# Cross attention and a top-4 expert layer on one core: the expert loop unrolled to 16 blocks a turn, with its stages two steps apart

## The chip, the cores and the metric

The kernel runs on one core of one Trainium2 chip (trn2). The metric is the device time of one execution in microseconds (us); lower is better. A change is told as a ratio of two such times.

## The reference, cut to what matters

The input is `x` of 4 x 1024 tokens with 256 features in float32, and a context of 4 x 77 tokens. One layer of cross attention (16 heads) is added to `x`; then comes the part that matters here, a feed-forward layer with 32 experts, of which each token picks 4, and one expert shared by all:

```python
T = B * S                                   # 4096 tokens
scores = softmax(xf @ Wg)                   # over E = 32 experts
weights, indices = top_k(scores, 4)
for e in range(E):
    tok, w = the tokens that chose e, and their weights      # at most 2048
    xg = xf[tok]
    out = silu(xg @ W1[e]) * (xg @ W3[e]) @ W2[e] * w[:, None]
    y = y.at[tok].add(out)
z = silu(xf @ Ws1) * (xf @ Ws3) @ Ws2
return x + y + z
```

Here D = 256, the inner width H = 128, and `W1`, `W3` are 256 x 128, `W2` is 128 x 256 for each expert. All matmuls are in float32, which the compiler splits, so that one product of 128 x 128 by 256 columns is two instructions on TensorE.

## The kernel before, in words

The kernel is written engine by engine: each engine has its own program, and they meet through counting semaphores alone. It has four parts in time: weights of the attention are folded together (up to about 165 us); attention, the second normalization, the router and the sending of each token's row into lists in HBM, one list per expert (to about 550 us); the shared expert, partly in between (to 584 us); and then two parts that matter here, the expert loop (586.6 to 888 us) and the sum of the four expert rows of each token (891 to 954 us).

**The expert loop** works on blocks of 128 rows of the lists, `BLOCKS` = 160 of them; which rows and which expert a block has stands in a table `tab` of three rows in SBUF (first row of the list, expert, column with the row numbers). One block passes these stages:

- SyncE loads the block's 128 rows from the list (`load_turn`, L525) into `xblk[:, q]`, one of `NX` = 8 buffers, 144 KB.
- TensorE transposes it (`block_T`, two transposes, L1235), and VectorE copies the result to `xbT` (`move_xbT`, L1186) and the 128 target row numbers to `yrow[:, q]` (L1188), which also has 8 columns.
- TensorE multiplies with `W1` and `W3` of the expert (`block_up`, four matmul instructions, L1467). ScalarE takes the silu of one half (`silu`, L831, into `eg`), VectorE multiplies with the other (`gate`, L1195, into `eh`).
- TensorE transposes `eh` (`block_hT`, L1235), VectorE copies it to `ehT` (`move_ehT`, L1202).
- TensorE multiplies with `W2` (`block_down`, two matmul instructions, L1481), ScalarE copies the result to `eo` (`move_eo`, L836), 8 buffers, and GpSimd sends its 128 rows of 1 KB by an indirect DMA to the rows `yrow` of `y_d` in HBM (`scatter_block`, L659).

So a block takes 9 matmul instructions on TensorE, each with a load of its weights.

**The order of the work** is written out by hand, by the helper `turns` (L319 to L332). Every engine runs through steps; in step q TensorE does `block_T` of block q, `block_up` of block q-1, `block_hT` of block q-2 and `block_down` of block q-3 (`LAG` = 3). VectorE does, in a step, `move_xbT` of q, `move_ehT` of q-2, `gate` of q-1; ScalarE does `silu` of q-1 and `move_eo` of q-3. A turn has `NX` = 8 steps. Turn 0 is written out, the turns 1 to 19 are a hardware loop (`Fori`), and the rest of the last blocks is written out behind it, so TensorE passes the end of a turn 20 times.

The transposed and intermediate buffers `xbT`, `eg`, `eh`, `ehT` have two copies each, and each stage has two of the eight PSUM banks. `move_xbT` of block b waits, through the semaphore `scattered[q]`, until the indirect DMA of block b-8 has landed, since `yrow` and `xblk` have eight places; `move_eo` waits for the same DMA, since `eo` has eight places. SyncE loads block b into `xblk` once block b-8 has been transposed and its row numbers copied.

In its turns 1 to 8, after the eight loads of the turn, SyncE also loads 512 KB of the shared expert's output from HBM (`base`, L536), which the final sum needs. Turn 9 is a loop of its own and so are the turns after it.

Of the kernel before, what the change touches and what calls it, by code (L numbers as in the profile page):

```python
# [17 lines left out]
I32 = mybir.dt.int32  # L18
U32 = mybir.dt.uint32
# [4 lines left out]
P = 128  # L24
# [6 lines left out]
def attention_moe_kernel(nc, x, ctx, Wq, bq, Wk, bk, Wv, bv, Wo, bo, gamma, beta,  # L31
# [46 lines left out]
    with ExitStack() as stack:  # L78
# [85 lines left out]
        tabf = sb("tabf", [P, 2, 3])  # L164
        tab = sb("tab", [3, LAG + BLOCKS + NX], I32)
        p1 = ExitStack()
# [151 lines left out]

        def turns(eng, stages, order, load_turn=None):  # L319

            def turn(i, qs, skip):
                of_turn = load_turn(i) if load_turn else None
                for q in qs:
                    for lag in order:
                        if not skip(q, lag):
                            stages[lag](i + (q - lag) // NX, (q - lag) % NX, of_turn and of_turn(q, lag))
# [64 lines left out]
        def _(sp):  # L392
# [125 lines left out]
            sp.wait_ge(s["tab_ready"], 1)  # L518
            rows_of = table(sp, "first_row", 0, LAG + NX, DUMMY)
# [23 lines left out]
            for q in range(NX):  # L543
                sp.wait_ge(scattered[q], 16 * TURNS)

# [23 lines left out]
        def _(pool):  # L569
# [93 lines left out]
            for q in range(NX):  # L663
                scatter_block(0, q)
            with pool.Fori(1, TURNS) as i:
                for q in range(NX):
                    scatter_block(i, q)
# [40 lines left out]
        def _(act):  # L708
# [117 lines left out]

            def silu(i, q, _):
# [5 lines left out]
            def move_eo(i, q, _):  # L833
                wait(act, scattered[q], i * 16)
                wait(act, "eo_psum", i * NX + (q + 1))
# [29 lines left out]
        def _(dve):  # L865
# [314 lines left out]

            def move_xbT(i, q, col):
                b = i * NX + q
# [3 lines left out]
                nc.vector.tensor_copy(xbT[:, q % 2, :, :].rearrange("p k n -> p (k n)"), bank(q % 2)[:, 0:D]  # L1186
                                      ).then_inc(s["xbT_sbuf"], 1)
                nc.vector.tensor_copy(yrow[:, q:q + 1], xblk[:, q, bass.ds(col, 1)].bitcast(U32)  # L1188
                                      ).then_inc(s["yrow_ready"], 1)

            def gate(i, q, _):
                b = i * NX + q
                wait(dve, "ehT_psum", b - 1)
                wait(dve, "eg_ready", b + 1)
                nc.vector.tensor_tensor(eh[:, q % 2, :], eg[:, q % 2, :], bank(2 + q % 2)[:, H:2 * H], ALU.mult  # L1195
                                        ).then_inc(s["eh_ready"], 1)

            def move_ehT(i, q, _):
                b = i * NX + q
                wait(dve, "eo_psum", b - 1)  # L1200
                wait(dve, "ehT_psum", b + 1)
                nc.vector.tensor_copy(ehT[:, q % 2, :], bank(4 + q % 2)[:, 0:P]).then_inc(s["ehT_sbuf"], 1)  # L1202

            turns(dve, {0: move_xbT, 1: gate, 2: move_ehT}, (0, 2, 1), table(dve, "y_col", 2, LAG + NX, ROW - 1))

# [24 lines left out]
        def _(pe):  # L1230
# [222 lines left out]

            def block_T(i, q, _):
                b = i * NX + q
                wait(pe, "xbT_sbuf", b - 1)
                wait(pe, ld_x[q], (i + 1) * 16)
                for k in range(KC):
                    last = transpose(bank(q % 2)[:, k * P:(k + 1) * P], xblk[:, q, k * P:(k + 1) * P])
                last.then_inc(s["xbT_psum"], 1)  # L1460

            def block_up(i, q, e):
                b = i * NX + q
                wait(pe, "eh_ready", b - 1)
                wait(pe, "xbT_sbuf", b + 1)
                for k in range(KC):
                    last = mm(bank(2 + q % 2)[:, 0:2 * H], xbT[:, q % 2, k, :],  # L1467
                              ew[:, bass.ds(e, 1), k * 2 * H:(k + 1) * 2 * H], start=k == 0, stop=k == KC - 1)
                last.then_inc(s["eh_psum"], 1)

            def block_hT(i, q, _):
                b = i * NX + q
                wait(pe, "ehT_sbuf", b - 1)
                wait(pe, "eh_ready", b + 1)
                transpose(bank(4 + q % 2)[:, 0:P], eh[:, q % 2, :]).then_inc(s["ehT_psum"], 1)

            def block_down(i, q, e):
                b = i * NX + q
                wait(pe, "eo_ready", b - 1)
                wait(pe, "ehT_sbuf", b + 1)  # L1480
                mm(bank(6 + q % 2)[:, 0:D], ehT[:, q % 2, :], ew[:, bass.ds(e, 1), 2 * D:3 * D], start=True, stop=True  # L1481
                   ).then_inc(s["eo_psum"], 1)
# [30 lines left out]
```

## Time and profile before

| what | value |
|---|---|
| time, median of 3 runs | 955.42 us |
| the 3 runs | 952.56, 4682.61, 955.42 us |
| the profiled execution: its span, first to last instruction of the program | 954.6 us |
| expert loop, from TensorE's first transpose to the end of the last indirect DMA's issue | 586.6 to 889.3 us |
| final sum | 891 to 954 us |

The table's first two lines are times without the profiler; for the profiled execution the page gives its span and no other time, and the span is 0.8 us below the median of the runs. PE is TensorE's matmul side, PEld its weight loads; a q behind an engine's name marks its sequencer (PEldq is TensorE's). A row of the timeline gives start, duration, engine, line, operation, names, count and, in brackets, the idle time before and what ended it; several like instructions can be merged into one row.

### The profile page before, as it was taken

To read this page: it belongs to the slowest core of one execution; us is meant where nothing else is said; L and a number is where in the kernel's file an instruction comes from. 1 tells how busy PE (TensorE), PEld (TensorE's weight loads), DVE (VectorE), ACT (ScalarE), POOL (GpSimd) and SP (SyncE) were. 2 spreads that over 40 slices of the span, in tenths; PEclk is the share of its full clock that TensorE was granted. 3 is DMA by queue.
4 is the path that set the end of the run, shared out by engine and by line. 5 is a ranking of instruction groups with operands and counts; after the bars stand their busy time and mean duration, and the time that the engine had idled before them with its cause. 6 is when DMAs were issued, how large, how long until landed. Compare 5 with 4: busy or idle time off the path is not lost.

```text
span 954.6 us, 17750 instructions
## 1 busy us (share of the span) xinstructions
PE 811.0 (85%) x3822; PEld 579.6 (61%) x3823; DVE 537.7 (56%) x1753; ACT 406.1 (43%) x1661; POOL 400.4 (42%) x397
## 2 busy tenths in 40 slices
PE   7877999999999999999689997898898898988100
PEld 4654666666666666666545655777777777777000
DVE  1763226667666767676847223555555555555588
ACT  1444767575757575757231111333333333333000
POOL 1201122247473737373852810455555545555100
PEclk9989999999999999999969999999999999999655
DMA  6245222234342425694393963656554444443799
GB/s 223 90 123 172 78 78 78 101 109 168 106 172 102 174 102 175 203 309 146 118 368 127 317 236 123 192 179 190 185 185 146 157 146 141 162 142 112 233 366 303
DMA packets 134396, 163.17 MB, mean 171 GB/s; under 512 B 11765, under 2 KB 121283, under 8 KB 134339
## 3 DMA queue, kind: packets, MB, share of 16 engines
q1 hardware_dynamic: 118595, 117.97, 39.7%
q0 software_dynamic: 15744, 44.62, 12.2%
q14 instruction: 43, 0.35, 0.1%
q8 instruction: 14, 0.23, 0.1%
HBM read 84.25 MB, written 78.27 MB: 170 GB/s over the span
## 4 chain that ended last, share of the span: by engine, by line
PE 73%; DMA 7%; DVE 7%; issue 5%; ACT 5%; SPq 0%; DVEq 0%; POOL 0%; POOLq 0%; ACTq 0%
PE psum L1321 15%; PE psum L1467 15%; PE psum L1235 11%; PE psum L1364 11%; PE psum L1481 7%; PE psum L1402 5%; ACT sm L768 4%; PE psum L1323 3%; DMA big<-y_d 3%; PE psum L1413 2%; DMA big<-in_x 2%; PE psum L1385 2%; DVE big L1217 2%; DMA pT<-xn2T_d 1%; DVE st L869 1%
## 5 line engine op out<-in xcount | busy, mean ns | idle before, releaser
L659 POOL DMA_INDIRECT y_d<-sm,yrow x160 | 155.1, 970 | 180.7 <-DVE yrow L1188 158.1
L1467 PE MATMUL psum<-big,xbT 128*128 x640 | 167.8, 385 | 1.3 <-DVE eh L1195 1.1
L1321 PE MATMUL psum<-big,xnT 128*128 (+2 forms) x384 | 157.2, 533 | 3.6 <-ACT sm L768 3.0
L768 ACT ACTIVATE sm<-psum,nmax 128x77 f32<-128x77 f32 x512 | 157.4, 371 | 0.0
L636 POOL DMA_INDIRECT expert_lists<-rows,slot x128 | 126.2, 986 | 59.4 <-issue 38.6
L618 POOL TENSOR_TENSOR sm<-sm,sinv 128x1232 f32<-128x1232 f32 x32 | 72.0, 2248 | 179.6 <-DVE sinv L1100 179.4
L1364 PE MATMUL psum<-big,pT 128*128 (+1 forms) x640 | 145.1, 383 | 2.0 <-DVE res L1091 2.0
L1364 PEld LDWEIGHTS psum<-big,pT 128*128 128x128 f32 x640 | 120.5, 192 | 17.0 <-DVE res L1091 2.1
L768 ACT ACTIVATION_READ_ACCUMULATOR sm<-psum,nmax 128x1 f32 x512 | 130.1, 254 | 0.1
L1467 PEld LDWEIGHTS psum<-big,xbT 128*128 128x128 f32 x640 | 109.7, 192 | 12.8 <-issue 2.3
L831 ACT ACTIVATE eg<-psum 128x128 f32<-128x128 f32 x160 | 44.4, 278 | 151.3 <-PE psum L1467 151.3
L1186 DVE COPY xbT<-psum 128x256 f32<-128x256 f32 x160 | 68.0, 425 | 57.7 <-PE psum L1235 46.5
L1481 PE MATMUL psum<-big,ehT 128*128 x320 | 95.7, 381 | 0.1
L1202 DVE COPY ehT<-psum 128x128 f32<-128x128 f32 x160 | 46.7, 292 | 85.5 <-PE psum L1235 83.9
L1321 PEld LDWEIGHTS psum<-big,xnT 128*128 128x128 f32 x384 | 65.9, 191 | 47.4 <-issue 42.3
L1235 PE MATMUL psum<-ident,xblk 128*128 128x128 f32 x320 | 62.5, 278 | 30.9 <-issue 30.9
L836 ACT ACTIVATE sm<-psum 128x256 f32<-128x256 f32 x160 | 61.3, 383 | 50.8 <-PE psum L1481 50.8
L1076 DVE TENSOR_REDUCE nmax<-psum 128x12 f32<-128x924 f32 x64 | 50.5, 794 | 53.1 <-PE psum L1323 53.0
L1235 PEld LDWEIGHTS psum<-ident,xblk 128*128 128x128 f32 x320 | 43.9, 142 | 52.9 <-issue 39.1
L1402 PE MATMUL psum<-pT,ws 128*128 128x512 f32 x128 | 64.0, 653 | 7.8 <-DMA pT<-xn2T_d 6.9
L1481 PEld LDWEIGHTS psum<-big,ehT 128*128 128x128 f32 x320 | 48.4, 191 | 12.4 <-issue 0.5
L1402 PEld LDWEIGHTS psum<-pT,ws 128*128 128x128 f32 x128 | 26.4, 210 | 38.5 <-issue 35.3
(181 smaller groups left out, 1061.5 us busy)
## 6 DMA issues: line engine op xcount, KB each, us to landing
xblk<-expert_lists SPq DMA_DIRECT2D x160, 144.0 KB, 2.2
y_d<-zero SPq DMA_DIRECT2D x32, 512.0 KB, 3.5
big<-y_d SPq DMA_DIRECT2D x32, 512.0 KB, 8.0
big<-in_L_ffn_W SPq DMA_DIRECT2D x16, 320.0 KB, 5.9
xin<-in_x SPq DMA_DIRECT2D x36, 128.0 KB, 2.1
expert_lists<-filler POOLq DMA_DIRECT2D x32, 144.0 KB, 3.9
big<-in_x SPq DMA_DIRECT2D x8, 512.0 KB, 3.5
xres<-in_x SPq DMA_DIRECT2D x8, 512.0 KB, 4.8
```

The source lines that it names most:

```text
L618: pool.tensor_tensor(e3, e3, sinv[:, t % 2, :].unsqueeze(2).to_broadcast([P, NH, SK]), ALU.mult).then_inc(s["probs_ready"], 1)
L636: pool.indirect_dma_start(out=lists, out_offset=bass.IndirectOffsetOnAxis(ap=slot[:, ph, tt, k:k + 1], axis=0), in_=rows[:, ph, tt, :], in ...
L659: pool.indirect_dma_start(out=y_d, out_offset=bass.IndirectOffsetOnAxis(ap=yrow[:, q:q + 1], axis=0), in_=eo[:, q, :], in_offset=None).the ...
L768: last = nc.scalar.activation(sm[:, t % 2, h * SK:(h + 1) * SK], head_scores(h, h + 1), ACT.Exp, bias=nmax[:, t % 2, h:h + 1], accum_out=s ...
L836: nc.scalar.activation(eo[:, q, :], bank(6 + q % 2)[:, 0:D], ACT.Copy).then_inc(s["eo_ready"], 1)
L1186: nc.vector.tensor_copy(xbT[:, q % 2, :, :].rearrange("p k n -> p (k n)"), bank(q % 2)[:, 0:D]).then_inc(s["xbT_sbuf"], 1)
L1235: return nc.tensor.transpose(out, in_, ident[0:n, 0:n])
L1321: mm(head_scores(h0, h1), xnT[:, t % 2, k, :], A[:, k, bass.ds(b, 1), cols], start=k == 0, stop=False)
L1364: last = mm(o_ps[:, 0:D], pT[:, to % 2, c, :], VO[:, bass.ds(batch(jo, po), 1), c, :], start=c == 0, stop=c == CK - 1)
L1402: last = mm(bank(2 * n + c), ws13[:, k, n * HS + c * P:n * HS + (c + 1) * P], xg[:, p, k, :], start=k == 0, stop=k == KC - 1)
L1467: last = mm(bank(2 + q % 2)[:, 0:2 * H], xbT[:, q % 2, k, :], ew[:, bass.ds(e, 1), k * 2 * H:(k + 1) * 2 * H], start=k == 0, stop=k == KC - 1)
L1481: mm(bank(6 + q % 2)[:, 0:D], ehT[:, q % 2, :], ew[:, bass.ds(e, 1), 2 * D:3 * D], start=True, stop=True).then_inc(s["eo_psum"], 1)
```

## The change

The steps of a turn become 16 and the stages are put two steps apart: `block_up` is done of block q-2, `block_hT` of block q-4 and `block_down` of block q-6 (`LAG` = 6). `xbT`, `eh` and `ehT` get four copies (`NB4`); `xblk`, `yrow`, `eo` keep eight, `eg` and the PSUM banks two. The waits for the reuse of `xbT`, `eh` and `ehT` are loosened accordingly. The table load takes `LAG + NTURN` = 22 registers. ScalarE and GpSimd keep turns of 8. TensorE, VectorE and SyncE now have 10 turns: turn 0 written out, 1 to 9 in loops. SyncE's `base` loads stay one per turn, in turns 1 to 8. The diff, cut to its core:

```diff
-    LAG = 3
-    TURNS = BLOCKS // NX
+    AT_UP, AT_HT, LAG = 2, 4, 6
+    NB4 = 4
+    NTURN = 16
+    TURNS = BLOCKS // NTURN
...
-        xbT = sb("xbT", [P, 2, KC, P])
+        xbT = sb("xbT", [P, NB4, KC, P])
         eg = sb("eg", [P, 2, H])
-        eh = sb("eh", [P, 2, H])
-        ehT = sb("ehT", [P, 2, P])
+        eh = sb("eh", [P, NB4, H])
+        ehT = sb("ehT", [P, NB4, P])
...
-            turn(0, range(NX), lambda q, lag: q < lag)
-            with eng.Fori(1, TURNS) as i:
-                turn(i, range(NX), lambda q, lag: False)
-            turn(TURNS, range(LAG), lambda q, lag: q >= lag)
+            turn(0, range(n), lambda q, lag: q < lag)
+            with eng.Fori(1, BLOCKS // n) as i:
+                turn(i, range(n), lambda q, lag: False)
+            turn(BLOCKS // n, range(LAG), lambda q, lag: q >= lag)
...
-                eng.reg_load(regs, tab[row:row + 1, bass.ds(i * NX, n)])
+                eng.reg_load(regs, tab[row:row + 1, bass.ds(i * NTURN, n)])
...
-                for q in range(NX):
-                    wait(sp, "xbT_psum", (i - 1) * NX + (q + 1))
-                    wait(sp, "yrow_ready", (i - 1) * NX + (q + 1))
-                    sp.dma_start(xblk[:, q, :], lists[bass.ds(of_turn(q, 0), P), :]).then_inc(ld_x[q], 16)
+                for q in range(NTURN):
+                    wait(sp, "xbT_psum", i * NTURN + (q + 1 - NX))
+                    wait(sp, "yrow_ready", i * NTURN + (q + 1 - NX))
+                    sp.dma_start(xblk[:, q % NX, :], lists[bass.ds(of_turn(q, 0), P), :]).then_inc(ld_x[q % NX], 16)
...
-            turns(act, {1: silu, LAG: move_eo}, (1, LAG))
+            turns(act, {AT_UP: silu, LAG: move_eo}, (AT_UP, LAG), NX)
...
-            def move_xbT(i, q, col):
-                b = i * NX + q
-                wait(dve, "eh_psum", b - 1)
-                wait(dve, scattered[q], i * 16)
+            def move_xbT(b, q, col):
+                x = q % NX
+                wait(dve, "eh_psum", b + (1 - NB4))
+                wait(dve, scattered[x], (b - x) * (16 // NX))
                 wait(dve, "xbT_psum", b + 1)
...
-                wait(dve, "ehT_psum", b - 1)
+                wait(dve, "ehT_psum", b + (1 - NB4))
...
-                wait(dve, "eo_psum", b - 1)
+                wait(dve, "eo_psum", b + (1 - NB4))
...
-            turns(dve, {0: move_xbT, 1: gate, 2: move_ehT}, (0, 2, 1), table(dve, "y_col", 2, LAG + NX, ROW - 1))
+            turns(dve, {0: move_xbT, AT_UP: gate, AT_HT: move_ehT}, (0, AT_HT, AT_UP), NTURN, table(dve, "y_col", 2, LAG + NTURN, ROW - 1))
...
-            turns(pe, {0: block_T, 1: block_up, 2: block_hT, LAG: block_down}, (0, 1, 2, LAG),
-                  table(pe, "expert", 1, LAG + NX, E - 1))
+            turns(pe, {0: block_T, AT_UP: block_up, AT_HT: block_hT, LAG: block_down}, (0, AT_UP, AT_HT, LAG), NTURN,
+                  table(pe, "expert", 1, LAG + NTURN, E - 1))
```

The waits that are not shown (`scattered` at the end of SyncE's part, the counts in `silu` and `move_eo`) name the same events in the new count of blocks.

## Rows read from the trace of the kernel before

**Rows 1.** Stretch view, one turn: span, PE, PEld, DVE, ACT, POOL (count), clock, DMA.
```profile
688.50:703.35 14.85, 13.38 (x73) 10.96 (x72) 7.79 (x33) 5.29 (x16) 7.75 (x9) 1.00 0.59 185
```

**Rows 2.** Chain that ended last, around two turn ends: start, us, what.
```profile
703.37 1.46 issue
704.83 0.43 PE psum L1235 x2
...
718.21 1.41 issue
```

**Rows 3.** Sequencers, by line: ns min/median/max, first and last start.
```profile
L330 PEldq ALU_OP  x1: 32/32/32, 702.3 to 702.3; - x1
...
L339 PEldq TENSOR_LOAD <-tab x21: 1376/1526/2186, 584.2 to 880.6; - x21
L339 SPq TENSOR_LOAD <-tab x20: 1147/1204/1582, 569.2 to 851.9; - x20
...
L647 POOLq TENSOR_LOAD <-fill_at x4: 1038/1084/1327, 523.9 to 544.9; - x4
...
L340 PEldq FUSED_REGOPS  x21: 85/180/180, 586.4 to 882.2; - x21
```

**Rows 4.** Timeline of one step on PE, DVE and ACT, and the next step's start.
```profile
699.95 0.38 PE L1235 MATMUL psum<-ident,xblk 128*128 128x128 f32 x2
...
700.37 0.43 DVE L1186 COPY xbT<-psum 128x256 f32<-128x256 f32 x1
...
701.62 0.28 DVE L1195 TENSOR_TENSOR eh<-eg,psum 128x128 f32<-128x128 f32 x1
...
701.58 0.38 PE L1235 MATMUL psum<-ident,xblk 128*128 128x128 f32 x2
...
701.84 0.38 ACT L836 ACTIVATE sm<-psum 128x256 f32<-128x256 f32 x1 [0.33 <-PE psum L1481]
```

**Rows 5.** Timeline of POOL, and the landing of the DMA issued at 694.88.
```profile
694.88 0.97 POOL L659 DMA_INDIRECT y_d<-sm,yrow  x1 [0.60 <-DVE yrow L1188]
...
703.07 0.97 POOL L659 DMA_INDIRECT y_d<-sm,yrow  x1 [0.66 <-DVE yrow L1188]
...
DMA to landing us min/median/max: 2.4/2.4/2.4
```

**Rows 6.** Timeline of SP and POOL at a `base` load; landings of L536 and of 688.22.
```profile
688.49 0.40 SPq L536 DMA_DIRECT2D base<-base_d  x1
...
688.22 0.97 POOL L659 DMA_INDIRECT y_d<-sm,yrow  x1 [0.66 <-DVE yrow L1188]
...
DMA to landing us min/median/max: 4.6/4.6/4.7
...
DMA to landing us min/median/max: 4.7/4.7/4.7
```

**Rows 7.** TensorE's clock: an idle stretch on PE and the stretch after it.
```profile
555.58 0.99 PE L1402 MATMUL psum<-pT,ws 128*128 128x512 f32 x1 [2.02 <-DMA pT<-xn2T_d]
...
555.80:559.20 3.40, 3.40 (x5) 1.34 (x5) 0.00 (x0) 0.00 (x0) 0.00 (x0) 0.51 0.86 322
```

**Rows 8.** Ends of a turn in two other loops: DVE's branches, next instructions, instructions a turn.
```profile
262.50:358.70 96.20, 95.63 (x453) 64.77 (x452) 65.77 (x197) 63.95 (x315) 54.20 (x43) 1.00 0.40 137
...
L303 DVEq COMPARE_BRANCH  x1: 63/63/63, 358.7 to 358.7; - x1
...
361.60 0.29 DVE L986 TENSOR_REDUCE lmax<-logits 128x4 f32<-128x128 f32 x1 [2.75 <-ACT logits L790]
...
921.60:935.90 14.30, 0.00 (x0) 0.00 (x0) 12.85 (x33) 0.00 (x0) 0.00 (x0) 0.50 1.10 366
...
L1224 DVEq FUSED_REGOPS  x1: 70/70/70, 921.8 to 921.8; - x1
```

**Rows 9.** Timeline of POOL, the last two indirect DMAs.
```profile
887.01 0.97 POOL L659 DMA_INDIRECT y_d<-sm,yrow  x1 [0.49 <-ACT sm L836]
888.29 0.97 POOL L659 DMA_INDIRECT y_d<-sm,yrow  x1 [0.30 <-issue]
```

More of the change, by code:

```diff
@@ L164, in attention_moe_kernel @@
         tabf = sb("tabf", [P, 2, 3])
-        tab = sb("tab", [3, LAG + BLOCKS + NX], I32)
+        tab = sb("tab", [3, LAG + BLOCKS + NTURN], I32)
         p1 = ExitStack()
@@ L317, in shared_rest, with turns @@
                     step(i, p)
-        def turns(eng, stages, order, load_turn=None):
+        def turns(eng, stages, order, n, load_turn=None):
             def turn(i, qs, skip):
@@ L326, in turn @@
                         if not skip(q, lag):
[L327 to L332 removed]
+                            stages[lag]((i + (q - lag) // n) * n + (q - lag) % n, (q - lag) % n,
+                                        of_turn and of_turn(q, lag))
+            turn(0, range(n), lambda q, lag: q < lag)
+            with eng.Fori(1, BLOCKS // n) as i:
+                turn(i, range(n), lambda q, lag: False)
+            turn(BLOCKS // n, range(LAG), lambda q, lag: q >= lag)
         def table(eng, name, row, n, max_val):
@@ L664, in _ @@
                 scatter_block(0, q)
-            with pool.Fori(1, TURNS) as i:
+            with pool.Fori(1, BLOCKS // NX) as i:
                 for q in range(NX):
@@ L831, in silu, with move_eo @@
                 nc.scalar.activation(eg[:, q % 2, :], bank(2 + q % 2)[:, 0:H], ACT.Silu).then_inc(s["eg_ready"], 1)
-            def move_eo(i, q, _):
-                wait(act, scattered[q], i * 16)
-                wait(act, "eo_psum", i * NX + (q + 1))
+            def move_eo(b, q, _):
+                wait(act, scattered[q], (b - q) * (16 // NX))
+                wait(act, "eo_psum", b + 1)
                 nc.scalar.activation(eo[:, q, :], bank(6 + q % 2)[:, 0:D], ACT.Copy).then_inc(s["eo_ready"], 1)
-            turns(act, {1: silu, LAG: move_eo}, (1, LAG))
+            turns(act, {AT_UP: silu, LAG: move_eo}, (AT_UP, LAG), NX)
         def rsqrt(dve, name, base, var, eps, w):
@@ L1452, in _, with block_T, block_up @@
             pe.wait_ge(s["z_added"], 2 * NG)
-            def block_T(i, q, _):
-                b = i * NX + q
+            def block_T(b, q, _):
+                x = q % NX
                 wait(pe, "xbT_sbuf", b - 1)
-                wait(pe, ld_x[q], (i + 1) * 16)
+                wait(pe, ld_x[x], (b - x) * (16 // NX) + 16)
                 for k in range(KC):
-                    last = transpose(bank(q % 2)[:, k * P:(k + 1) * P], xblk[:, q, k * P:(k + 1) * P])
+                    last = transpose(bank(q % 2)[:, k * P:(k + 1) * P], xblk[:, x, k * P:(k + 1) * P])
                 last.then_inc(s["xbT_psum"], 1)
-            def block_up(i, q, e):
-                b = i * NX + q
+            def block_up(b, q, e):
                 wait(pe, "eh_ready", b - 1)
@@ L1466, in block_up, with block_hT, block_down @@
                 for k in range(KC):
-                    last = mm(bank(2 + q % 2)[:, 0:2 * H], xbT[:, q % 2, k, :],
+                    last = mm(bank(2 + q % 2)[:, 0:2 * H], xbT[:, q % NB4, k, :],
                               ew[:, bass.ds(e, 1), k * 2 * H:(k + 1) * 2 * H], start=k == 0, stop=k == KC - 1)
                 last.then_inc(s["eh_psum"], 1)
-            def block_hT(i, q, _):
-                b = i * NX + q
+            def block_hT(b, q, _):
                 wait(pe, "ehT_sbuf", b - 1)
                 wait(pe, "eh_ready", b + 1)
-                transpose(bank(4 + q % 2)[:, 0:P], eh[:, q % 2, :]).then_inc(s["ehT_psum"], 1)
-            def block_down(i, q, e):
-                b = i * NX + q
+                transpose(bank(4 + q % 2)[:, 0:P], eh[:, q % NB4, :]).then_inc(s["ehT_psum"], 1)
+            def block_down(b, q, e):
                 wait(pe, "eo_ready", b - 1)
                 wait(pe, "ehT_sbuf", b + 1)
-                mm(bank(6 + q % 2)[:, 0:D], ehT[:, q % 2, :], ew[:, bass.ds(e, 1), 2 * D:3 * D], start=True, stop=True
+                mm(bank(6 + q % 2)[:, 0:D], ehT[:, q % NB4, :], ew[:, bass.ds(e, 1), 2 * D:3 * D], start=True, stop=True
                    ).then_inc(s["eo_psum"], 1)
-            turns(pe, {0: block_T, 1: block_up, 2: block_hT, LAG: block_down}, (0, 1, 2, LAG),
-                  table(pe, "expert", 1, LAG + NX, E - 1))
+            turns(pe, {0: block_T, AT_UP: block_up, AT_HT: block_hT, LAG: block_down}, (0, AT_UP, AT_HT, LAG), NTURN,
+                  table(pe, "expert", 1, LAG + NTURN, E - 1))
 TAB_OPS = 21
```

21 lines of the change are left out of this document (9 added, 12 removed).

## Prediction

> **What bounds the kernel now.** I read the page first: TensorE is the busiest engine, and the chain that ended last runs through it for most of the span, in the expert loop for all of it. So the loop's turns come next. A turn of 8 blocks [rows 1] has TensorE's matmuls busy for 13.38 of 14.85 us at clock 1.00; VectorE has 7.79, so no other engine is near a bound. The chain [rows 2] shows one hole a turn: 1.46 us of "issue", where TensorE waits for no other engine; from one hole's start to the next it is 718.21 - 703.37 = 14.84 us. Inside a turn TensorE has no hole: the transposes of two neighbouring blocks start at 699.95 and 701.58 [rows 4], 1.627 us apart (steps of 1.62 and 1.63 alternate), and PE isn't idle between them. So a step is TensorE's own work, and a turn's end costs 14.84 - 8 x 1.627 = 1.82 us, a little more than the hole, and 20 ends cost 36.4 us. What fills the hole is on TensorE's sequencer [rows 3]: it counts the loop at 702.3, branches, loads 11 registers (1.526 us, median) and computes with them (0.180 us); the first weight load comes about 2.5 us behind 702.3. About 0.7 us of this is hidden by what was handed over before.
>
> **Turn ends, part by part.** The change has 10 ends instead of 20. Each load now takes 22 registers. The trace has no such load, so I bound it: GpSimd loads 8 in 1.084 us and SyncE 11 in 1.204 [rows 3], 0.04 us for each further register, which gives +0.44 for 11 more; in proportion to the count it would be +1.53. I take 0.06 a register, nearer to the row with the slope, so +0.66, and for L340 +0.13 (0.180 for 11, 0.085 in the last turn, where three are used, so 0.012 a register): +0.79 in all, bounds +0.57 and +1.7. The hand-over gains 0.2 us, as worked out below. An end then costs 1.82 + 0.79 - 0.2 = 2.4, ten cost 24: **-12.4 us** (bounds -14 to -3).
>
> The Trainium skill has a dearer rule (Runtime: NRT & Kernel Launch, Instruction fetch mechanics): about 200 ns for each register loaded, even in bulk. The trace disagrees at 11 registers, 1.526 us where the rule gives 2.2. By the rule's slope 11 more would be +2.2 us and ten ends some 15 us more than in my sum.
>
> **The stages two steps apart.** Inside a turn TensorE is already full, so spacing can't speed up a step. It could bring something at a turn's end alone: the sequencer could run further ahead. What it does to the ring of 8 buffers, which stays, is worse. In a step whose transposes start at 0 (699.95), VectorE copies `xbT` at 0.42, `gate` ends at 1.95, `move_eo` ends at 2.27 [rows 4], and the indirect DMA starts at 3.12 (703.07) and lands 2.4 later, at 5.5 [rows 5]. The copy of block b waits for the landing of block b-8. Before, block b-8 has its step of `block_down` at b-5, so the landing is at 5.5 and the copy at 5 x 1.627 + 0.42 = 8.55: 3.05 us to spare (rows 5 and 4: issued at 694.88, landed 697.3, copy of the eighth block after it at 700.37). With `LAG` = 6 that step is at b-2: the copy could be at 2 x 1.627 + 0.42 = 3.67, but the landing is at 5.5. Every copy is 1.83 us late. Two steps of spacing nearly absorb this. Step b+2 needs, before its `block_up`, `gate` of b-2, which VectorE does behind the late copy: 5.5 + 0.1 to start, 1.0 for copy, row numbers, `ehT` and `gate` (700.37 to 701.9 without its waits), 0.1 and 0.25 for the sequencer is 6.95 from the start of step b-2. That must fit in 4 steps and 0.2: 4P = 6.75, P = 1.69 instead of 1.627. Where the turn's end lies within the four steps it gives the time back, so I count 12 of 16 steps in 9 turns: 108 x 0.06 = **+6.5 us** (bounds 0 and +14). As `gate` comes that late, the sequencer is held as before and gains only 0.2 us at the end of a turn; without the ring it would gain 1.3 (its last wait would be for `move_eo` of two steps ago, 2 x 1.627 - 2.27 = 0.98 us ahead of the step's start, instead of for the last `gate`, 1.95 - 1.627 = 0.32 us behind it).
>
> **What was hidden by the 3.05 us.** In eight turns a 512 KB `base` load lies in the queues for 4.6 us, and the indirect DMA beside it lands after 4.7 instead of 2.4 [rows 6]. Before, 3.05 + the turn's end covered that. Now there is no spare, and the base load is issued in the middle of a turn (right behind the load that waits for the row numbers of the turn's block 7), while two indirect DMAs are under way or start; the later landing, +1.0 to +2.3 us, goes straight into TensorE. 8 x 1.5 = **+12 us** (bounds 0 and +18).
>
> **Start, end, clock.** The first table load lies open (TensorE starts with it): +0.8. At the end, the last blocks' `block_down` come 0.54 us apart, but GpSimd needs 887.01 to 888.29 = 1.28 for each indirect DMA [rows 9]; with six blocks instead of three to drain, the last is issued some 1.2 us later: together **+2 us**. The granted clock is 1.00 with holes of 1.46 us [rows 1, 2]. After a hole of 2.02 us it was 0.5 (1.2 of 2.4 GHz) for 3.4 us [rows 7], which costs 1.7. The new hole is 1.46 + 0.79 - 0.2 = 2.05. I take that it falls at two or three of ten ends: **+4 us** (bounds 0 and +17). SyncE's own end of turn and its later stores of `base` run 8 blocks (13 us) ahead and cost nothing; VectorE's own load starts about a step behind TensorE's, and two steps of cover absorb that. Eight and four buffers in SBUF cost no time.
>
> **Sum.** -12.4 + 6.5 + 12 + 2 + 4 = +12.1 us on a span of 954.6: 966.7, or on the median, 0.8 higher, **967.5 us**.
>
> **Rivals.**
> - B, the ring doesn't bind: the landing comes earlier than the trace says, or the copy isn't held. Then the sequencer's lead of 1.3 counts: ten ends of 1.82 + 0.79 - 1.3 = 1.31, saving 36.4 - 13.1 = 23.3, less 2 for start and end: 955.4 - 21.3 = 934.1. For it: the purpose of two steps of cover. Against: rows 4 and 5 leave no room for 6 steps and a landing in 8.
> - C, the ring binds but `base` loads don't hit (the delayed landing falls on a block with cover from the turn's end): 967.5 - 12 = 955.5. For it: the hit depends on tenths of a us; against: two indirect DMAs start in any 3.3 us.
> - D, slower by over 2%: the turn's end decides. Above a hole of about 2 us the clock falls at every end, 10 x 1.7 = 17 instead of 4, and with the hits at 2 us (+16 instead of 12) it is 984.5. It begins to win where the load of 22 registers takes over about 2.3 us.
> - E, the longer body doesn't stay in the instruction store: at the end of a turn of the attention loop (197 VectorE instructions a turn) VectorE branches at 358.7 and starts its next instruction at 361.60, 2.75 us idle; in the final sum (33 a turn) the next sequencer instruction starts 0.2 us behind the branch [rows 8]. The new body has 64, nearer to 33. If it missed, 9 x 2.75 = 25 more: 992. TensorE's body of 144 matmuls is below the 453 of the attention turn, which shows no hole.
>
> The Trainium skill's rule here (same page and section) is that a branch to a page that is no longer in the engine's small window waits for a fetch; the VectorE rows agree that there is such a wait of some 2.7 us, and leave open from which size.
>
> **Chances.** A (forecast) 0.43, of which 0.05 above 974.5; B 0.07; C 0.22; D 0.23; E 0.05. The kernel's measurement can tell about 2% (19 us) from no change: faster 0.07 (B), same 0.38 + 0.22 = 0.60, slower 0.05 + 0.23 + 0.05 = 0.33. The range, 947 to 987, leaves out B and most of E.
>
> **What would show it.** 10 holes of about 2 us on TensorE instead of 20 of 1.46; TENSOR_LOAD of 2.2 us; steps of `block_T` at 1.627 with some longer ones, mean near 1.69; VectorE's `xbT` copy starting 2.2 us, not 0.42, after the transposes, released by the indirect DMA; a step of over 3 us in the middle of turns 1 to 8 and none in turn 9; 0.5 in the clock behind some ends. Steps of 1.627 throughout and a copy at 0.42 would refute the ring; mid-turn holes missing, the hits.

## The result, and the profile after

The changed kernel takes 978.94 us (median of four runs, 976.60 to 980.12), the kernel before 955.66 us on the same chip (median of four, one of which, 4682.61 us, is far from the rest). The ratio is 1.025, with a 95% interval of 1.0228 to 1.0271: slower by 23.3 us, about twice the 12 us forecast, and above the 2% that the prediction took as what can be told from no change.

The profiled execution has a span of 978.1 us against 954.6. First its page: busy time by engine, the chain that ended last, and the costliest group on VectorE.

```profile
PE 829.8 (85%) x3822; PEld 586.9 (60%) x3823; DVE 523.6 (54%) x1753; ACT 406.5 (42%) x1661; POOL 401.2 (41%) x397
...
PE 56%; DMA 17%; issue 9%; DVE 8%; ACT 6%; POOL 3%; DVEq 1%; POOLq 1%; SPq 1%; ACTq 0%
PE psum L1321 15%; PE psum L1364 11%; DMA y_d<-sm,yrow 9%; PE psum L1235 8%; PE psum L1466 7%; PE psum L1402 4%; ACT sm L771 4%; POOL y_d L662 3%; DMA big<-y_d 3%; PE psum L1323 3%; PE psum L1478 3%; DMA big<-in_x 2%; PE psum L1413 2%; PE psum L1385 2%; DVE big L1217 1%
...
L1188 DVE COPY xbT<-psum 128x256 f32<-128x256 f32 x160 | 67.7, 423 | 166.8 <-DMA y_d<-sm,yrow 121.2
```

The reader is to see `DMA y_d<-sm,yrow` in the chain with 9% of the span. VectorE was idle for 166.8 us ahead of the 160 copies of `xbT`, and 121.2 of them ended with the landing of an indirect DMA. In the kernel before the same group (there L1186) reads:

```profile
L1186 DVE COPY xbT<-psum 128x256 f32<-128x256 f32 x160 | 68.0, 425 | 57.7 <-PE psum L1235 46.5
```

The stretch view answers to [rows 1]; its columns are the same. These are two neighbouring turns of 16 blocks, 31.70 and 30.62 us, where two turns of 8 took 29.7.

```profile
644.87:676.57 31.70, 28.46 (x145) 21.76 (x145) 13.86 (x64) 10.60 (x32) 15.99 (x17) 1.00 0.51 162
676.57:707.19 30.62, 27.85 (x144) 21.97 (x145) 14.11 (x64) 10.59 (x32) 15.56 (x17) 1.00 0.49 158
```

The sequencers' table loads, now of 22 registers, answer to [rows 3]:

```profile
L342 PEldq TENSOR_LOAD <-tab x11: 1934/2040/2210, 581.7 to 899.8; - x11
L342 SPq TENSOR_LOAD <-tab x10: 1620/1880/2131, 567.5 to 856.7; - x10
```

The timeline around a `base` load answers to [rows 4 to 6]. To be seen: each copy of `xbT` is ended by the DMA, and starts 0.76 to 0.92 us behind the transposes of the next block, where it used to start 0.42 behind its own. At 692.20 the `base` load goes out, VectorE then stands idle for 1.74 us, the copy at 695.29 starts 3.4 us behind its transposes, and TensorE's next transposes wait for it.

```profile
689.37 0.42 DVE L1188 COPY xbT<-psum 128x256 f32<-128x256 f32 x1 [1.01 <-DMA y_d<-sm,yrow]
...
690.08 0.38 PE L1235 MATMUL psum<-ident,xblk 128*128 128x128 f32 x2
690.84 0.42 DVE L1188 COPY xbT<-psum 128x256 f32<-128x256 f32 x1 [0.60 <-DMA y_d<-sm,yrow]
...
692.20 0.40 SPq L539 DMA_DIRECT2D base<-base_d  x1
692.67 0.42 DVE L1188 COPY xbT<-psum 128x256 f32<-128x256 f32 x1 [0.95 <-DMA y_d<-sm,yrow]
...
695.29 0.42 DVE L1188 COPY xbT<-psum 128x256 f32<-128x256 f32 x1 [1.74 <-DMA y_d<-sm,yrow]
695.77 0.44 PE L1235 MATMUL psum<-ident,xblk 128*128 128x128 f32 x2 [0.41 <-DVE xbT L1188]
```

In the next turn the same hit is larger, and the granted clock falls behind it (timeline, then the stretch at 0.50):

```profile
723.45 0.40 SPq L539 DMA_DIRECT2D base<-base_d  x1
...
728.05 0.42 DVE L1188 COPY xbT<-psum 128x256 f32<-128x256 f32 x1 [3.43 <-DMA y_d<-sm,yrow]
728.54 0.44 PE L1235 MATMUL psum<-ident,xblk 128*128 128x128 f32 x2 [2.10 <-DVE xbT L1188]
```

```profile
729.51:732.92 3.41, 3.41 (x12) 2.59 (x11) 1.57 (x8) 0.66 (x2) 0.00 (x0) 0.50 0.51 142
```

A turn's end, on TensorE's timeline, with its hole of 2.15 us, answers to [rows 2]. The bracket names a copy of VectorE, but TensorE's sequencer is in its table load until 706.4 and computes with the registers until 706.9:

```profile
704.44 0.60 PE L1478 MATMUL psum<-big,ehT 128*128 x2
707.19 0.43 PE L1235 MATMUL psum<-ident,xblk 128*128 128x128 f32 x2 [2.15 <-DVE xbT L1188]
```

**Where the 23 us are.** A step is the time from a block's transposes to the next block's; a full one is 1.63 us. From the first block's transposes to the last block's the kernel before takes 293.0 us and the changed one 314.65. Summing what each step has above 1.63 us by its place in the turn gives, in us (step 0 goes from the transposes of a turn's first block to those of its second; an end is step 15 with steps 0 and 1 behind it, in turns of 8 step 7 with those two):

| | before | after | difference |
|---|---|---|---|
| turns' ends (19; 9), without falls of the clock | 34.5 | 21.6 | -12.9 |
| steps 2 to 9, 13 and 14 of a turn | 0 | 7.9 | +7.9 |
| steps 10 to 12 (place of the `base` load), without falls | 0 | 15.7 | +15.7 |
| six falls of the clock, three at ends, three in steps 10 to 12, 1.75 each | 0 | 10.5 | +10.5 |
| first turn, rounding | -0.7 | -0.3 | +0.4 |
| last transposes to last indirect DMA | 8.6 | 12.9 | +4.3 |
| start of the loop's first block | 586.6 | 584.2 | -2.4 |

The sum is +23.5 us. The final sum behind the last indirect DMA is the same in both, 66.3 us. The 1.75 us for a fall is an estimate from turns' ends with and without one, below. The parts repeat, the falls do not: a second trace of the changed kernel (`after_again`, below) has by the same sums 21.6 us at ends, 9.8 in steps 2 to 9, 13 and 14, 15.6 in steps 10 to 12, and four falls instead of six, 7.0 us.

Of the 15.7 us, 3.4 stand in turn 7, at block 122, together with one of the falls. An experiment below shows that these stay when the `base` load of that turn is moved away. The `base` loads of the other turns thus go with 12.1 us and two falls (turn 9, which has no such load, has the other 0.2).

### The profile page after: what moved, and what is told of

Its sections match the earlier page's. It is cut to its first block, busy times and chain, and to the rows that moved or that the text cites. A ratio compares the mean times of both kernels' runs of the same rounds, so it can differ in the third digit from the quotient of the medians.

```text
span 978.1 us, 17716 instructions
## 1 busy us (share of the span) xinstructions
PE 829.8 (85%) x3822; PEld 586.9 (60%) x3823; DVE 523.6 (54%) x1753; ACT 406.5 (42%) x1661; POOL 401.2 (41%) x397
## 4 chain that ended last, share of the span: by engine, by line
PE 56%; DMA 17%; issue 9%; DVE 8%; ACT 6%; POOL 3%; DVEq 1%; POOLq 1%; SPq 1%; ACTq 0%
PE psum L1321 15%; PE psum L1364 11%; DMA y_d<-sm,yrow 9%; PE psum L1235 8%; PE psum L1466 7%; PE psum L1402 4%; ACT sm L771 4%; POOL y_d L662 3%; DMA big<-y_d 3%; PE psum L1323 3%; PE psum L1478 3%; DMA big<-in_x 2%; PE psum L1413 2%; PE psum L1385 2%; DVE big L1217 1%
## 5 line engine op out<-in xcount | busy, mean ns | idle before, releaser
L1466 PE MATMUL psum<-big,xbT 128*128 x640 | 177.1, 401 | 3.7 <-DVE eh L1196 1.5
L1188 DVE COPY xbT<-psum 128x256 f32<-128x256 f32 x160 | 67.7, 423 | 166.8 <-DMA y_d<-sm,yrow 121.2
L1364 PEld LDWEIGHTS psum<-big,pT 128*128 128x128 f32 x640 | 120.6, 192 | 17.5 <-DVE res L1093 2.0
L1466 PEld LDWEIGHTS psum<-big,xbT 128*128 128x128 f32 x640 | 113.1, 197 | 22.4 <-issue 11.1
L1478 PE MATMUL psum<-big,ehT 128*128 x320 | 98.5, 391 | 0.1
L1235 PE MATMUL psum<-ident,xblk 128*128 128x128 f32 x320 | 64.7, 285 | 33.4 <-DVE xbT L1188 23.8
L1402 PE MATMUL psum<-pT,ws 128*128 128x512 f32 x128 | 60.7, 623 | 6.7 <-DMA pT<-xn2T_d 5.8
L1202 DVE COPY ehT<-psum 128x128 f32<-128x128 f32 x160 | 45.1, 282 | 14.5 <-PE psum L1235 14.3
L731 ACT ACTIVATE xnT<-psum 128x256 f32<-128x256 f32 x33 | 12.6, 383 | 85.9 <-PE psum L1235 85.9
```

Of the source, the lines that this page charges most:

```text
L1188: nc.vector.tensor_copy(xbT[:, q % NB4, :, :].rearrange("p k n -> p (k n)"), bank(q % 2)[:, 0:D]).then_inc(s["xbT_sbuf"], 1)
L1235: return nc.tensor.transpose(out, in_, ident[0:n, 0:n])
L1364: last = mm(o_ps[:, 0:D], pT[:, to % 2, c, :], VO[:, bass.ds(batch(jo, po), 1), c, :], start=c == 0, stop=c == CK - 1)
L1402: last = mm(bank(2 * n + c), ws13[:, k, n * HS + c * P:n * HS + (c + 1) * P], xg[:, p, k, :], start=k == 0, stop=k == KC - 1)
L1466: last = mm(bank(2 + q % 2)[:, 0:2 * H], xbT[:, q % NB4, k, :], ew[:, bass.ds(e, 1), k * 2 * H:(k + 1) * 2 * H], start=k == 0, stop=k == K ...
L1478: mm(bank(6 + q % 2)[:, 0:D], ehT[:, q % NB4, :], ew[:, bass.ds(e, 1), 2 * D:3 * D], start=True, stop=True).then_inc(s["eo_psum"], 1)
```

## The experiments

The theory after the result: VectorE's wait for the scatter (the indirect DMA into `y_d`) of block b-8, placed ahead of the copy of block b, makes a ring that is too short for a block's longer way. It costs three times, as direct lateness, as hits of the `base` loads, and by holding TensorE's sequencer back at a turn's end. The rivals: the turn's end with its larger load and the clock (D), and the distance of the stages as such.

The experiments ran on other chips, where the kernel before took 980 to 991 us; in every trace from there the parts ahead of the loop are longer (its first block starts at 606 to 622 us instead of 584 to 587), and the final sum is 66.2 to 66.4 us as here. So medians are compared as ratios to the kernel before on the same chip, and the loop by its own length in the trace. The kernel before has its only trace on the first chip, 293.0 us; how far that length holds on the others is judged by the changed kernel alone, 314.65 there and 312.3 on one of them.

**Sixteen places for the row numbers.** The ring alone is changed.

```
-        yrow = sb("yrow", [P, NX], U32)
+        yrow = sb("yrow", [P, NTURN], U32)
-                wait(dve, scattered[x], (b - x) * (16 // NX))
+                wait(dve, scattered[x], (b - x) * (16 // NX) - 16)
-                nc.vector.tensor_copy(yrow[:, x:x + 1], ...
+                nc.vector.tensor_copy(yrow[:, q:q + 1], ...
```

GpSimd's loop has 16 blocks a turn for it, with `eo[:, q % NX]` and `scattered[q % NX]`.

> The changed kernel with 16 places for the row numbers instead of 8 (the copy of block b then waits for the indirect DMA of block b-16, not b-8); everything else as in the change. Ring theory (the 8 places bind once block_down comes six steps behind): the copy starts 0.42 us behind the transposes again, steps are 1.63 us, TensorE's sequencer runs ahead, and an end of a turn costs 1.82 + 0.6 - 1.3 = 1.1 us; 955.7 - 36.4 + 11 + 2 = 932 us, with TensorE's clock at full speed in the whole loop. Rival (the ends of the turns, dearer by the load of 22 registers and the lower clock behind them, are what costs): the ring gives back at most its 6 to 10 us, 970 us.

Measured: 976.16 us, ratio 0.9891 (0.9846 to 0.9936), and 0.9813 (0.9749 to 0.9878) when it ran again on another chip. The loop is 275.6 us. The stretch view of a turn, the group of the copies, and TensorE's timeline at a turn's end:

```profile
699.05:726.38 27.33, 26.41 (x145) 21.96 (x145) 15.37 (x64) 10.59 (x32) 15.55 (x16) 1.00 0.58 184
```

```profile
L1188 DVE COPY xbT<-psum 128x256 f32<-128x256 f32 x160 | 67.9, 424 | 54.5 <-PE psum L1235 18.6 <-DMA y_d<-sm,yrow 14.5 <-issue 6.1
```

```profile
723.67 0.38 PE L1235 MATMUL psum<-ident,xblk 128*128 128x128 f32 x2
723.89 1.03 PE L1466 MATMUL psum<-big,xbT 128*128 x4
724.75 0.27 PE L1235 MATMUL psum<-ident,eh 128*128 128x128 f32 x1
724.86 0.60 PE L1478 MATMUL psum<-big,ehT 128*128 x2
726.38 0.43 PE L1235 MATMUL psum<-ident,xblk 128*128 128x128 f32 x2 [0.92 <-issue]
```

The waits for the DMA fall from 121.2 to 14.5 us. In turns 1 to 4 every step between the ends is 1.63 us, although the `base` loads go out in them as before. The hole at the end is 0.92 us instead of 2.15, though the load is as long:

```profile
L342 PEldq TENSOR_LOAD <-tab x1: 2101/2101/2101, 723.5 to 723.5; - x1
```

It starts at 723.5, just as TensorE begins the last step, of which 1.9 us of work are handed over. In the changed kernel the load began at 704.4 and TensorE's last matmuls of the turn at 704.44, since the sequencer had been held by the late copy:

```profile
L342 PEldq TENSOR_LOAD <-tab x1: 2051/2051/2051, 704.4 to 704.4; - x1
```

So one ring accounts for the direct lateness, nearly all hits, and the long ends; and behind the loop's first four blocks the clock stays at 1.00 in this trace. (In the second trace it fell twice, in turn 7 and at its start.) The loop is 39 us shorter than the changed kernel's. This is more than the ring had been charged with, and the ratio was still worse than expected: the kernel gains 17.4 us in the loop and gives 3.2 back in the drain (11.87 us instead of 8.64), together the 14.0 us between the medians. I had set the ends and the drain too low in the expectation.

**The two parts alone, one ring of 8.** Turns of 16 with the stages one step apart:

```
-    AT_UP, AT_HT, LAG = 2, 4, 6
+    AT_UP, AT_HT, LAG = 1, 2, 3
```

> The changed kernel with the stages one step apart again (up, hT and down at 1, 2 and 3 steps), turns of 16 and four buffers kept. Ring theory: no copy waits for an indirect DMA; ten ends of about 1.82 + 0.6 = 2.4 us are 12 us less than twenty of 1.82; if the clock falls behind six of them, as in the changed kernel, 10 us come back: 943 to 953 us. Rival (turn ends are what costs in the changed kernel): slower than before, 965 us or more.

Measured: 996.8 us, ratio 1.0069 (1.0041 to 1.0096), slower where a gain was expected. Its profiled execution, 1004.18 us, is the slowest of its ten, 7.4 above the median; its loop is 304.9 us. The table load takes 19 registers here. A turn whose start has a fall of the clock, the stretch of the fall at the next turn's start, and a turn without one:

```profile
682.19:712.73 30.54, 28.09 (x145) 23.02 (x145) 15.58 (x64) 10.59 (x32) 15.56 (x16) 0.94 0.52 163
714.06:717.46 3.40, 3.40 (x12) 2.65 (x11) 0.97 (x4) 0.71 (x3) 0.89 (x1) 0.50 0.17 46
743.02:773.90 30.88, 27.35 (x145) 22.00 (x145) 15.48 (x64) 10.26 (x32) 15.65 (x17) 1.00 0.52 161
```

```profile
712.73 0.43 PE L1235 MATMUL psum<-ident,xblk 128*128 128x128 f32 x2 [2.45 <-issue]
```

The hole at an end is 2.0 to 2.45 us now, and behind seven of nine ends the clock is 0.5 for one stretch of 3.4 us. The last step of a turn and the next two add up to 9.37 us with the fall (at 712.73) and to 7.57 without (at 773.90), so a fall costs 1.8 us (seven ends with a fall take 9.26 us in the mean, the two without 7.54). This is rival D's mechanism, seen here alone. Nine ends cost 23.3 us without the falls, where 19 cost 34.5; seven falls take 12.6 back, and steps within the turns another 8.9, all of it in the two turns that begin without a fall, near their `base` load, and at block 122, where the eighth fall is.

Stages two apart with turns of 8:

```
-    NTURN = 16
+    NTURN = 8
```

> The changed kernel with turns of 8 again, stages two steps apart and four buffers kept (the table load takes 14 registers). Ring theory: copies wait for the indirect DMAs of eight blocks ago, steps get longer between the ends, and nothing is saved at the ends: 958 to 968 us. Rival (the 16-block turn is what costs): 954 to 957 us, as before.

Measured: 1003.63 us, ratio 1.0127 (1.0085 to 1.0168), loop 305.5 us. The ratio is at the upper end of what the ring was expected to cost; the clock never falls, and no hole on TensorE is above 1.7 us.

**Work for TensorE in the hole.** Four products of 256 columns at each turn's end, into an unused half of a bank, so that TensorE is not idle while the load runs:

```
+            def fill_hole(i):
+                wait(pe, "eo_ready", i * NTURN + (NTURN - LAG - 1))
+                for _ in range(4):
+                    mm(bank(6)[:, D:2 * D], ident[:, :], ew[:, 0, 0:D], start=True, stop=True)
```

> The changed kernel with four more matmuls (128 x 128 by 256 columns, float32, into unused columns of a PSUM bank, 1.73 us of TensorE's time together) at the end of each full turn, ahead of the branch, so that TensorE works while its sequencer loads the table. Their results are not used. Clock theory (about six falls of the granted clock in the loop cost 1.7 us each, 10 us of the changed kernel's 23): no stretch at 0.5 behind a turn's end, and 969 to 973 us. Rival (the clock costs nothing, since the ring sets the pace): 978 us or more.

Measured: 1013.46 us, ratio 1.0238 (1.0197 to 1.0278), the same as the changed kernel (1.025, and 1.0242 below). The falls at ends are gone (turn starts in turns 1 to 8 have 1.7 us above full steps instead of 4.9), but the ends themselves grew from 20.1 to 22.7 us in all, and the three falls in steps 10 to 12 are still there. Holding the clock at the ends in this way pays nothing; as the added work lengthens the ends, the run doesn't isolate what the falls there cost.

**The base loads moved away.** The changed kernel with all eight behind the last load of a block; it was measured beside the changed kernel itself.

```
                 load_turn(i, rows_of(i))
-                sp.dma_start(base[:, bass.ds((i - 1) * TG, TG), :], ...
...
+            for i in range(NG):
+                sp.dma_start(base[:, i * TG:(i + 1) * TG, :], ...
             sp.wait_ge(s["eo_psum"], BLOCKS)
```

> The changed kernel once more, as the measure for its neighbours on this chip. Ratio to the kernel before 1.020 to 1.030; in its trace 310 to 318 us from the first block's transposes to the last block's (314.65 in its first trace, 293.0 in the kernel before). Every theory expects the same here; a length outside these bounds would say that the loop differs between chips by more than what is to be told apart.

> The changed kernel with the eight loads of base taken out of the turns and issued behind the last load of a block; the ring of 8 places stays. Theory (a base load holds back a scatter's landing, and the ring of 8 passes that on to TensorE): in the first trace steps 10 to 12 of the turns lie 21.0 us above 1.63 us a step, these go, and the clock's falls that began there go too; the loop comes to 290 to 296 us, the ratio to 1.001 to 1.009, with 0 to 3 us given back where the final sum waits for base. Rival 1 (the long steps 10 to 12 are the ring's own, the base load is a bystander): loop 310 or more, ratio 1.02 or more. Rival 2 (the falls of the clock come from the turn's end alone): 5 us less gain, ratio 1.009 to 1.014.

Measured: the changed kernel again 1012.66 us, ratio 1.0242 (1.0193 to 1.0290), loop 312.3. With the loads moved 1012.56, ratio 1.0248 (1.0192 to 1.0303), loop 312.4. The total is what the first rival expected, yet its reason does not hold: in turns 1 to 8 steps 10 to 12 fell from 17.2 to 7.0 us above full steps. Of the 7.0, 5.2 stand in turn 7, at block 122, with a fall of the clock. There the copy comes as late with no `base` load under way (second line) as in the changed kernel (first line), so this one is not a hit of the load:

```profile
827.14 0.42 DVE L1188 COPY xbT<-psum 128x256 f32<-128x256 f32 x1 [4.24 <-DMA y_d<-sm,yrow]
```

```profile
854.46 0.42 DVE L1189 COPY xbT<-psum 128x256 f32<-128x256 f32 x1 [4.13 <-DMA y_d<-sm,yrow]
```

The rest of the cost moved. In the last turn, where the eight loads now go out, the excess rose from 0.8 to 7.8 us, with a fall of the clock that lasted 6.8 us (timeline):

```profile
913.82 8.93 SPq L544 DMA_DIRECT2D base<-base_d  x8
...
918.54 0.42 DVE L1189 COPY xbT<-psum 128x256 f32<-128x256 f32 x1 [3.33 <-DMA y_d<-sm,yrow]
```

More came back in steps 13 and 14 (+3.0) and in the first turn (+1.7), which I cannot ascribe to the edit. So the loads do cause the long steps in the turns other than 7, and moved to this place they save nothing, since they meet scatters there too.

**The way shortened by one step.** The down product one step behind `hT`, so that a scatter goes out one step earlier; first with 8 places, then with 16.

```
-    AT_UP, AT_HT, LAG = 2, 4, 6
+    AT_UP, AT_HT, LAG = 2, 4, 5
```

> The changed kernel with the down product one step behind the transpose of the hidden rows instead of two (steps 0, 2, 4, 5), so that a block's scatter is issued one step of 1.63 us earlier; 8 places as before. Theory (the copy of block b waits for the landing of the scatter of block b-8, which lay 1.8 us behind in my sum): nearly all of that lateness goes; between hits the steps are 1.63 us, the hits of the base loads shrink by up to 1.6 us each, the turn's end from 3.9 to about 2.8 us; loop 280 to 292 us, ratio 0.985 to 1.003. Rival (the greater distance of the stages itself costs, by more data under way or by the filling and draining of six stages, and the ring is a bystander): loop 308 or more, ratio 1.015 or more. Rival 2 (only the first lateness goes, the hits of the base loads stay whole): loop 298 to 304.

> Sixteen places for the row numbers and the down product one step behind: both cures of the ring together. Theory: the ring was gone already with 16 places (loop 275.6 us, nothing above 1.63 us within the turns but four odd steps), so the second cure takes only one block of 1.3 us off the drain behind the last step and nothing off the loop: 274 to 278 us, ratio 0.985 to 0.991. Rival (with 16 places landings still bind at times, and were the four odd steps): loop 271 to 273, ratio 0.982 to 0.985. Rival 2 (two steps between the last two stages are what keeps TensorE's sequencer ahead of the engine at a turn's end; without them an end costs 2.6 us instead of 1.3): loop 286 to 290, ratio 1.000 to 1.004.

Measured with 8 places: 992.59 us, ratio 1.0023 (0.9999 to 1.0046), loop 294.8, 17.5 us shorter than its neighbour. In turns 1 to 8 steps 2 to 9 lie at 1.63 us (7.5 us of excess gone), while steps 10 to 12 keep 14.2 of 17.2, falls included and 4.8 of it in turn 7: the first lateness goes, a hit stays larger than the slack. That lies between the theory's figure and its second rival's. With 16 places: 980.92 us, ratio 0.9913 (0.9887 to 0.9938), loop 283.3, longer than the 275.6 with the stages two apart. The difference is at the ends, 16.8 instead of 11.6 us over nine, the hole there 1.63 instead of 0.92:

```profile
699.85 0.43 PE L1235 MATMUL psum<-ident,xblk 128*128 128x128 f32 x2 [1.63 <-issue]
```

So two steps between the last two stages do keep the sequencer ahead, by 0.6 us an end; the second rival had the direction, and twice the size.

**The wait taken off the path, with both lengths of the turn.** Eight places again, but wait and copy of the row numbers behind `gate`, two steps later:

```
             def move_xbT(b, q, _):
                 wait(dve, "eh_psum", b + (1 - NB4))
-                wait(dve, scattered[x], (b - x) * (16 // NX))
                 wait(dve, "xbT_psum", b + 1)
...
             def gate(b, q, col):
...
+                wait(dve, scattered[x], (b - x) * (16 // NX))
+                nc.vector.tensor_copy(yrow[:, x:x + 1], xblk[:, x, bass.ds(col, 1)].bitcast(U32)
+                                      ).then_inc(s["yrow_ready"], 1)
```

> The changed kernel with its 8 places, but VectorE's wait for the scatter of block b-8 and the copy of the row numbers behind it taken from step 0 to behind the gate product of step 2, so that the wait comes 3.26 us later and the copy of the block's columns no longer stands behind it. Theory (the ring of 8 is what held the loop up, and its lateness was 1.8 us plus 1 to 2 us at a base load): 3.26 us more is enough nearly everywhere; loop 272 to 281 us as with 16 places (275.6), ratio 0.985 to 0.994. Rival (16 places helped by something else, as GpSimd's turn of 16 or the other place of the counters): loop 300 or more, ratio 1.01 or more. Rival 2 (the block's columns now stay in xblk two steps longer, and the loads of blocks become late instead): loop 282 to 300, with TensorE waiting for xblk.

> The same with turns of 8: stages two apart and a ring that doesn't bind, which leaves the length of the turn as the only difference to its neighbour late_yrow. Theory (with stages two apart TensorE's sequencer is 1.9 us ahead of the engine when a turn ends, so that of the load of 14 registers, 1.45 us, nothing is left and of the branch and the addresses, 0.9 us, some 0.4): 19 ends of 0.6 us, loop 269 to 276 us, ratio 0.981 to 0.990; the turn of 16 brings nothing then. Rival (an end costs as much as with the turn of 16, about 1.4 us, whatever it loads): loop 284 to 290, ratio 0.997 to 1.004, and the longer turn is worth its registers.

> Sixteen places once more, beside its neighbours of this call: ratio 0.985 to 0.993, loop 274 to 278 us (275.6 in its first trace).

Measured, turns of 16: 965.97 us, ratio 0.983 (0.9764 to 0.9897), loop 276.2; the 16 places beside it 0.9813 (0.9749 to 0.9878), loop 276.0. Two different cures of the ring agree within 0.6 us of loop, so it was not GpSimd's turn of 16 that helped. In its loop TensorE waited only once, 1.2 us, for a block's load. The wait that was moved guards `yrow` alone: the scatter does not read `xblk`, unlike what the section on the kernel before says. Turns of 8: 958.96 us, ratio 0.9795 (0.972 to 0.9869), loop 269.6. Two of its turns, and the start of a turn on TensorE with the load that lies ahead of it:

```profile
659.52:672.99 13.47, 13.40 (x73) 10.97 (x73) 7.51 (x34) 5.29 (x16) 7.76 (x9) 1.00 0.63 204
672.99:686.45 13.46, 13.37 (x73) 10.93 (x73) 7.52 (x34) 5.29 (x16) 7.77 (x9) 1.00 0.66 208
```

```profile
671.12 0.38 PE L1235 MATMUL psum<-ident,xblk 128*128 128x128 f32 x2
671.34 1.03 PE L1466 MATMUL psum<-big,xbT 128*128 x4
672.20 0.27 PE L1235 MATMUL psum<-ident,eh 128*128 128x128 f32 x1
672.31 0.60 PE L1478 MATMUL psum<-big,ehT 128*128 x2
672.97 0.43 PE L1235 MATMUL psum<-ident,xblk 128*128 128x128 f32 x2
```

```profile
L342 PEldq TENSOR_LOAD <-tab x1: 1412/1412/1412, 671.0 to 671.0; - x1
```

A turn of 8 takes 13.46 us instead of 14.85 [rows 1], with the same 13.4 us of matmuls. The load of 14 registers starts as the last step does and is over before it; what is left of an end is 0.45 us in these turns and 0.58 in the mean of all 19, against 1.3 to 1.5 with 22 registers, and 19 such ends (11.1 us) are shorter than 9 of those. This version ran once more:

> The version that the runs point to (turns of 8, stages two apart, row numbers copied at step 2) once more in more rounds, since its first interval is wide: ratio 0.977 to 0.986, loop 267 to 272 us (269.6 in its first trace, 293.0 in the kernel before). The theory is that the gain is the 23 us of the loop less some 4 us of a longer drain; a ratio of 0.99 or more would say that the start or the end of the loop takes back more than that.

Measured: 962.0 us, ratio 0.9807 (0.9766 to 0.9847), loop 269.8. It beats the kernel before by 1.9% (interval 1.5 to 2.3%) and, by the two ratios, the changed kernel by 4.3%.

All loop lengths side by side, in us from the first block's transposes to the last block's:

| | turn of 8 | turn of 16 |
|---|---|---|
| stages one step apart, ring of 8 | 293.0 (before) | 304.9 |
| two apart, wait ahead of the copy, ring of 8 | 305.5 | 314.7, 312.3 (after) |
| two apart, ring of 16 places | not tried | 275.6, 276.0 |
| two apart, ring of 8, wait two steps later | 269.6, 269.8 | 276.2 |

In each row that has both, the longer turn is the slower one, by 7 to 12 us; the 12 compares traces from two chips.

## Why the prediction was wrong

Its mechanisms were right in kind. It was wrong about the outcome because the clock's term was too small (4 us where 10.5 were measured) and because no term stood for a hold-up of 3.4 us at block 122. By its own steps:

- **Turn ends, -12.4 us.** 20.1 us of last steps and 6.8 of first ones, less three falls, are 21.6 us for nine ends, 2.40 each where 2.4 was forecast, so the term held. The load of 22 registers took 2.04 us (median) where I took 2.19, so 11 more cost 0.05 us each, between the 0.04 read from [rows 3] and the 0.06 taken. That is partly luck: across the runs the time doesn't rise evenly with the count (last section).
- **The ring, +6.5 us.** Measured +7.9. The copies start on the landing, 2.46 us behind their transposes (median) where the sum had 2.25, instead of 0.42. That the stages gain the sequencer nothing under the ring held too.
- **The hits, +12 us.** Steps 10 to 12 have 15.7 us without the clock's falls, of which 12.1 go with `base` loads. Eight hits of 1.5 us were forecast; five were 1.1 to 1.8, but in turns 4 and 5 they took 2.6 and 3.2, the copy 5.2 us behind its transposes in the one (the line at 728.05). So the term held in sum, though not in its even size. The other 3.4 us, in turn 7, come from the hold-up at block 122, which the prediction had no term for and whose cause is open.
- **The clock, +4 us: mis-sized, and the largest miss.** It measured 10.5. Of the ends alone three had a fall, as forecast; three more fell in steps 10 to 12, behind holes of 2.10 to 2.91 us on TensorE: two at hits of the `base` load, one at block 122. The sum had looked for long holes at ends only. One term made the other dearer, and I had added them as if they were independent. The number of falls differs between executions: the second trace of the same kernel has four.
- **Start and end, +2 us.** The drain cost 4.3 instead of 1.2; with the ring open it is still 3.2. The first block began 2.4 us earlier, for a reason that no run shows. Together +1.9.

The misses are 6.5 on the clock, 3.7 in steps 10 to 12 (nearly all of it block 122), 1.4 on the ring and -0.5 on the ends, 11 in all: 23 instead of 12. Rival B's reason (the ring doesn't bind) was false for this kernel, but its price was good: it gave 1.31 us for an end under a free sequencer, and the 16 places show 1.3 to 1.5. Its 934.1 us is a ratio of 0.978; measured were 0.989 and 0.981. Rival C is refuted by the hits. Rival D expected falls at all ends and 984.5 us; the time came near it, the place of the falls did not. Rival E is out: with 16 places the body is as long and the hole at a turn's end is 0.92 us, less than one fetch of the 2.7 us of [rows 8]. VectorE's sequencer, too, goes on 0.23 to 0.26 us behind each of its eight branches back in the changed kernel.

The Trainium skill's figure for register loads (Runtime: NRT & Kernel Launch, Instruction fetch mechanics), about 200 ns each, does not hold for the added ones: 11 more cost 0.5 us. The page speaks of registers loaded from HBM; the table here lies in SBUF.

What I did not ask in the prediction was whether each half of the change would pay alone. The runs say that the stages two apart are worth 23 to 29 us of loop once the ring is open, and that the turn of 16 costs 7 to 12 us at either distance. In the sum the turn of 16 stood as a gain of 12.4 us; against turns of 8 with the same stages it is none.

## What to carry to other kernels

When stages are pulled apart, count every ring that spans them, in time from issue to landing and not in blocks: the buffers that were doubled here were not the ones that bound, and moving one wait two steps back, off the path of the data it didn't guard, was worth 4% against the changed kernel (ratios 0.983 and 1.0242). Slack that a loop loses does not only cost its own lateness; it also lets in disturbances that were there before and invisible (a 512 KB load beside scatters), and behind two of them the clock fell. Here the longer unrolled turn was the dearer way to hide its end: a sequencer one step ahead of its engine left 0.45 us of an end with a load of 1.42 us, and 1.3 us with one of 2.1.

## What the runs showed of the hardware

- A table load on TensorE's sequencer takes, as medians of a trace, 1.53 us for 11 registers, 1.42 to 1.47 for 14, 2.15 for 19, 1.79 to 1.81 for 21 and 2.01 to 2.18 for 22. It is no even function of the count.
- In the run with turns of 16 and stages one apart the granted clock fell behind seven of nine ends, whose holes on TensorE are 2.0 to 2.45 us, and behind one hole of 1.91 within a turn; the two ends without a fall had 2.21 and 2.32. In the first trace with 16 places a hole of 1.85 us had none, in the second one of 1.85 had one, and another fall came behind two holes of 0.37 and 1.36. So the length of the hole alone does not decide. A fall lasted 3.4 us at 0.5 (1.2 of 2.4 GHz), one 6.8, and one of 3.4 cost 1.8 us.
- The kernels with turns of 16 have one hold-up of TensorE at blocks 122 to 126, also with the `base` loads moved away (a step of 4.70 us), with stages one apart (5.31) and where the ring is open (4.38 with the later wait, 3.70 with 16 places). With 16 places and `LAG` = 5 it is 4.94. The kernel before has no step above 1.63 us there but the turn's end, the kernels with turns of 8 and stages two apart have none above 2.5. The cause stays open.
